# Four-layer token kernel on one core: inverse roots of layer 0 moved from GpSimd to ScalarE, a shorter QR step, LayerNorm products on GpSimd, rotations spread over three MLP groups

## The chip, the cores and the metric

The kernel runs on one core of one Trainium2 chip. The metric is the device time of one execution in microseconds (us); less is better. Five engines each work through an instruction list of their own: TensorE (PE, with its weight loads as PEld), VectorE (DVE), ScalarE (ACT), GpSimd (POOL) and SyncE (SP), which starts the DMAs. They meet only through semaphores.

## The reference, cut to what matters

The input `x` holds 32 sequences ("tiles" below) of 128 tokens with 144 channels. Four stages follow one another:

```python
def layer0(x, c):                                  # layers 2 and 3 are built alike
    sh_a, sc_a, g_a, sh_m, sc_m, g_m = split(swish(c) @ w_mod + b_mod, 6)
    q, k, v = heads((ln(x) * (1 + sc_a) + sh_a) @ w_qkv + b_qkv)      # 16 heads of 9
    q, k = ln(q, g_q), ln(k, g_k)                  # layer 0 alone: a LayerNorm within each head
    o = softmax(q @ k.T * 9 ** -0.5) @ v
    x = x + g_a * (o @ w_proj + b_proj)
    h = gelu((ln(x) * (1 + sc_m) + sh_m) @ w1 + b1)
    return x + g_m * (h @ w2 + b2)

def layer1(x, cond):                               # the rotations
    U, _ = qr(P)                                   # P is 144 x 64
    R = expm(skew(silu(cond) @ W.T + b))           # one 64 x 64 matrix per sequence
    z = x @ U
    return x + (z @ R - z) @ U.T
```

Layer 2 is attention and MLP without the LayerNorm of q and k; layer 3 has the same attention and a mixture of four experts, two per token.

## The kernel before, in words

The 32 tiles stay on the chip in `X`. Each layer takes them one by one through attention, and in groups of four through the MLP (8 groups a layer). The stages of one tile are, by their names in the code: `ln` and `xh` (LayerNorm statistics and product, for two tiles at a time), `xt` and `xe` (transpose, modulate), `qkv`, `v` (copies out of PSUM), in layer 0 `n1` and `n2` (the LayerNorm of q and k; its means are taken out of the weights beforehand, so that only an inverse root is left), `h1`, `r1` (split in a high and a low part), `qt`, `kt` (transposes), `s1`, `mx` (scores and their maximum), `s2`, `ex` (scores again, exponential), `pv`, `oe` (weighted values), `pj`, `py` (projection, gate). A group's MLP is `mln`, `mxh`, `mxt`, `mxe`, `mxs`, `up`, `ue` (gelu), `dn`, `de`.

Beside layer 0 run three further pieces of work. The QR of `P` is 64 Householder steps, each dependent on the one before: `qb` on PE broadcasts a row (L1831), `qc` on ACT copies it to `VS` and sums its squares (L1198, L1199), `q1` is a dot product and a sign on DVE (L1550, L1551) and the root of the sum on POOL by `pow` (L998), `q2` is six linked DVE instructions (L1558 to L1567). After the 64 steps a chain of small products (`qm` to `qu`, L1842 to L1862 on PE, L1572 to L1591 on DVE) makes U. The matrix exponential is 12 squarings (`sq`, L1907 on PE, L1003 on POOL, L1231 on ACT, L1632 on DVE). A rotation (`rxt` to `re`, for four tiles; L1795 to L1821 on PE) needs U, the exponential, and the finished layer 0 of its four tiles; layer 2 of a tile needs its rotation. There are eight rotations, placed by the table `ROTS`: two behind MLP group 6, six behind group 7.

The inverse roots of q and k are made in `n1`: DVE sums the squares (L1374) and scales them (L1376), POOL raises 128x32 numbers to the power -0.5 (L962), DVE multiplies (L1383, L1386). The LayerNorm products are made in part on DVE (128 channels, L1277) and in part on POOL (the last 16 channels, three times, L931).

The order of the instructions on each engine is made when the program is built. `order()` gives every stage a place on a common scale of tiles from the tables PAIR, TILE, GROUP, EXPERT, STEP and START; `plan()` then walks through all engines with costs of its own for each instruction (class `Probe`) and lets each engine take, among its stages that are ready, the one with the lowest place. Each engine's list is fixed from then on. Where PE would have nothing to do in that plan, it puts in filler products of `eye` with `eye`, whose result nobody reads (stage `hum`, L1666). The plan counts one table load of ACT (1300 in its costs) when an exponential follows a gelu or the reverse. ACT_TABLE_LOAD instructions themselves are put in when the program is compiled.

```python
                elif stage == "q2":
                    ...
                    link(e.scalar_tensor_tensor(SH[:, k:k + 1], sc[:, 2:3], -1.0, sc[:, 1:2], ALU.add, ALU.mult))
                    after()
                    link(e.scalar_tensor_tensor(sc[:, 4:5], VS[:, 0:1], SH[:, k:k + 1], sc[:, 0:1], ALU.mult, ALU.add))
                    link(e.scalar_tensor_tensor(sc[:, 6:7], T1[:, k:k + 1], SH[:, k:k + 1], sc[:, 6:7], ALU.mult, ALU.add))
```

## Time and profile before

| | us |
|---|---|
| median of 3 runs (1365.66 to 1374.56) | 1369.18 |
| the profiled execution | 1369.59 |
| its span in the trace | 1367.7 |

The span is the time from the first to the last instruction that the profiler saw; 1.9 us lie around it. Busy time of an engine is the time in which at least one of its instructions ran; the fillers of PE count as busy. PEclk is the TensorE clock that was granted, as a share of full speed. Each row of a group of instructions names its line in the kernel, its engine, the tiles it writes and reads (`s_` in SBUF, `p_` in PSUM, buffer numbers left out), the count, the busy time and the mean duration of one, and the idle time of the engine just before them with what ended it.

### The profile page before, as it was taken

How to read it: one execution, taken by the hardware profiler on the slowest of the kernel's cores; microseconds unless marked ns; L12 is line 12 of the kernel's file. 1: busy time of each engine (PE TensorE's matmuls, PEld its weight loads, DVE VectorE, ACT ScalarE, POOL GpSimd, SP SyncE). 2: the span in 40 equal slices, each digit the busy share in tenths (PEclk: the TensorE clock that was granted, in tenths of full speed). 3: DMA queues.
4: the chain of work that ended last, by engine and by line, in shares of the span. 5: the costliest groups of instructions: out<-in, count | busy, mean ns of one | idle time of the engine just before them, and what ended most of it. 6: DMA issues, size and time to landing. Idle time of an engine off the chain costs nothing. (4 is left out here: it accounts for less than half of the span.)

```text
span 1367.7 us, 36454 instructions
## 1 busy us (share of the span) xinstructions
PE 1285.6 (94%) x13444; PEld 1069.1 (78%) x13444; DVE 957.7 (70%) x2820; ACT 910.3 (67%) x1792; POOL 666.9 (49%) x782
## 2 busy tenths in 40 slices
PE   8898989999999999998999999999999999999998
PEld 7467767777788877676877778778888889888897
DVE  6788788878888746688677777776666656655341
ACT  3664867757767636666776775677867776776641
POOL 5757788988988321132333333244353342515331
PEclk9999989989899899999899999999999999999999
DMA  6321111111121101143121222221111111111100
GB/s 187 95 86 31 44 43 44 47 37 43 37 60 48 54 24 44 45 124 79 59 69 58 65 64 67 58 77 42 37 57 35 53 42 48 53 34 58 44 12 22
DMA packets 98069, 76.15 MB, mean 56 GB/s; under 512 B 25536, under 2 KB 83179, under 8 KB 97766
## 3 DMA queue, kind: packets, MB, share of 16 engines
q1 hardware_dynamic: 97894, 73.83, 19.0%
q8 instruction: 108, 1.77, 0.5%
q14 instruction: 67, 0.55, 0.1%
HBM read 43.27 MB, written 28.95 MB: 53 GB/s over the span
## 5 line engine op out<-in xcount | busy, mean ns | idle before, releaser
L1788 PE MATMUL p_B<-s_pC,s_H 128*128 128x144 f32 x1900 | 250.4, 288 | 0.9 <-ACT s_FA L1020 0.8
L1408 DVE TENSOR_REDUCE s_MX<-p_S 128x16 f32<-128x2048 f32 x96 | 219.4, 2286 | 38.6 <-PE p_S L1720 37.6
L1788 PEld LDWEIGHTS p_B<-s_pC,s_H 128*128 128x128 f32 x1900 | 239.9, 190 | 7.0 <-issue 2.0
L1117 ACT ACTIVATE s_Pm<-p_S 128x2048 f32<-128x2048 f32 x96 | 180.2, 1878 | 25.1 <-PE p_S L1734 24.5
L962 POOL TENSOR_TENSOR s_s<-s_s,s_half 128x32 f32<-128x32 f32 x32 | 175.0, 5471 | 17.2 <-DVE s_s L1376 16.9
L1168 ACT ACTIVATE s_H<-p_B,s_pC 128x512 f32<-128x512 f32 (+1 forms) x207 | 137.8, 686 | 61.5 <-PE p_B L1654 60.2
L958 POOL TENSOR_TENSOR s_OC<-s_OC,s_RB 72x256 f32<-72x256 f32 x96 | 70.6, 736 | 191.1 <-DMA s_RB<-sums 191.0
L1519 DVE SCALAR_TENSOR_TENSOR s_CQ<-p_B,s_rw,s_CQ 128x144 f32<-128x144 f32 x128 | 41.1, 363 | 115.1 <-PE p_B L1788 114.5
L966 POOL TENSOR_TENSOR s_X<-s_X,s_GA 128x144 f32<-128x144 f32 x96 | 48.5, 505 | 138.2 <-DVE s_GA L1427 138.1
L1660 PE MATMUL p_B<-s_eye,s_QK 128*128 128x128 f32 x768 | 111.1, 282 | 2.8 <-ACT s_JS L1199 1.0
L1660 PEld LDWEIGHTS p_B<-s_eye,s_QK 128*128 128x128 f32 x768 | 88.3, 144 | 15.2 <-issue 5.3
L931 POOL TENSOR_SCALAR s_XHA<-s_X,s_MVA,s_VEA 128x48 f32<-128x48 f32 x96 | 52.9, 561 | 88.4 <-PE p_B L1694 87.2
L1743 PE MATMUL p_B<-s_Pm,s_VA 128*32 128x128 f32 x2560 | 90.7, 285 | 1.6 <-ACT s_Pm L1117 0.4
L1654 PE MATMUL p_B<-s_XMh,s_WFh 128*128 128x512 f32 x207 | 90.3, 436 | 0.2 <-DVE s_XMs L1464 0.2
L1654 PE MATMUL p_B<-s_XMl,s_WFh 128*128 128x512 f32 x207 | 82.8, 400 | 0.0
L1654 PE MATMUL p_B<-s_XMs,s_WFs 80*128 80x512 f32 x207 | 82.8, 400 | 0.0
L1654 PE MATMUL p_B<-s_XMh,s_WFl 128*128 128x512 f32 x207 | 82.4, 398 | 0.0
L1743 PEld LDWEIGHTS p_B<-s_Pm,s_VA 128*32 128x32 f32 x2560 | 67.9, 113 | 13.8 <-issue 4.7
L1720 PEld LDWEIGHTS p_S<-s_KT,s_QT 27*128 27x128 f32 x1536 | 51.5, 188 | 33.6 <-ACT s_Pm L1117 17.1
L1734 PEld LDWEIGHTS p_S<-s_QT,s_KT 29*128 29x128 f32 x1536 | 52.6, 191 | 29.7 <-issue 13.2
L1720 PE MATMUL p_S<-s_KT,s_QT 27*128 27x128 f32 x1536 | 64.9, 286 | 9.9 <-ACT s_Pm L1117 8.3
L976 POOL TENSOR_TENSOR s_X<-s_X,s_GM 128x288 f32<-128x288 f32 x48 | 38.5, 808 | 72.4 <-DVE s_GM L1511 36.2
(318 smaller groups left out, 3214.8 us busy)
## 6 DMA issues: line engine op xcount, KB each, us to landing
heads<-s_OT SPq DMA_DIRECT2D x96, 256.0 KB, 2.3
s_GM<-gates SPq DMA_DIRECT2D x48, 144.0 KB, 3.2
s_GA<-gates SPq DMA_DIRECT2D x96, 72.0 KB, 3.0
s_OC<-heads SPq DMA_DIRECT2D x192, 36.0 KB
s_RB<-sums SPq DMA_DIRECT2D x192, 36.0 KB
s_QT<-s_MS SPq DMA_DIRECT2D x192, 8.0 KB
s_SG<-in_main SPq DMA_DIRECT2D x33, 72.0 KB, 2.2
out<-s_X SPq DMA_DIRECT2D x8, 288.0 KB, 3.6
```

Of the source, the lines that this page charges most:

```text
L931: e.tensor_scalar(XH[:, k, 128:208].rearrange("p (a c) -> p a c", c=16)[:, 0:5:2, :], X[:, b, 128:144].unsqueeze(1).to_broadcast([128, 3, ...
L958: e.tensor_tensor(OC[n % 2][0:72, :], OC[n % 2][0:72, :], RB[n % 2][:, :], ALU.mult).then_inc(SEM["ml"], 1)
L962: e.tensor_tensor(s32[n % 2][:, 3, :], s32[n % 2][:, 2, :], half[:, :], ALU.pow).then_inc(SEM["n1p"], 1)
L1117: e.activation(Pm[n % 2][:, :], bank["s2", i][:, :], ACT.Exp, scale=SCALE).then_inc(SEM["ex"], 1)
L1168: e.activation(hb[0:n, to, :], bank["up", i][0:n, :], ACT.Gelu_apprx_tanh, bias=b1[l][0:n, 5 * x + to:5 * x + to + 1]).then_inc(SEM["ge"], 1)
L1408: e.tensor_reduce(MX[n % 2][:, :], bank["s1", i][:, :].rearrange("p (h k) -> p h k", h=NH), AX.X, ALU.max, negate=True).then_inc(SEM["mx"], 1)
L1654: r = e.matmul(o, x if swap else y, y if swap else x, start=(j == 0), stop=(j == 3))
L1660: r = e.transpose(bk[:, 128 * j:128 * j + 128], QK[n % NQK][:, c:c + 128].bitcast(F32), eye[:, :])
L1720: ins = e.matmul(bk[:, c:c + 128], QT[n % NT][q, j, :], KT[n % NT][q, j, :], start=True, stop=True)
L1734: ins = e.matmul(bk[:, c:c + 128], KT[n % NT][q, j, :], QT[n % NT][q, j, :], start=True, stop=True)
L1743: ins = e.matmul(bk[32 * r:32 * r + 32, 128 * j:128 * j + 128], VA[n % NVA][:, h, :], Pm[n % 2][:, 512 * r + 128 * j:512 * r + 128 * j + 1 ...
L1788: ins = e.matmul(bk[:, 256 * i2:256 * i2 + C], hb[0:n, c, 128 * t:128 * t + 128], w2[l][0:n, 5 * x + c, :], start=(c == 0), stop=(c == 4))
```

## The change

- **Inverse roots of q and k (layer 0).** DVE only sums the squares. DVE then makes one Newton step for 1/sqrt in three linked instructions (L1429 to L1433). POOL has no part in it.
- **A 1x1 logarithm** (`lnz`) stands at the start of ACT's program and, in layer 0, ahead of the first softmax exponential or `n1` that follows a gelu.
- **QR step.** ACT sums the squares first (of half the values) and then copies; POOL's root waits only for the sum and writes `SH` itself; the sign goes to a column of `GO` and, with a factor of 0.5, into `sc[:, 2:4]`; `q2` falls from six linked instructions on DVE to four. VS and T1 lie in one tile, so that a single instruction takes both numbers.
- **LayerNorm products of layer 0** (both LayerNorms, 64 products of 128 channels) go from DVE to POOL. Layers 2 and 3 keep them on DVE.
- **Squaring.** POOL's factor 2.0 is read from memory and is no immediate.
- **Rotations.** `ROTS` puts three behind MLP group 5, two behind 6 and three behind 7.
- **Order.** All place tables have new numbers, and two per layer (first and last tile) in place of one; some of the planner's costs are changed (what DVE and POOL cost each other).

```diff
-ROTS = {6: (0, 1), 7: (2, 3, 4, 5, 6, 7)}
+ROTS = {5: (0, 1, 2), 6: (3, 4), 7: (5, 6, 7)}
...
-        more = {ACT.Exp: 95, ACT.Gelu_apprx_tanh: 110, ACT.Identity: 175, ACT.Square: 50 if accum_out is None else 90}[func]
-        return self.part(80 + more + 0.78 * cols(o), {ACT.Exp: "exp", ACT.Gelu_apprx_tanh: "gelu"}.get(func))
+        more = {ACT.Exp: 95, ACT.Ln: 95, ACT.Gelu_apprx_tanh: 110, ACT.Identity: 175, ACT.Square: 50 if accum_out is None else 90}[func]
+        return self.part(80 + more + 0.78 * cols(o), {ACT.Exp: "exp", ACT.Ln: "exp", ACT.Gelu_apprx_tanh: "gelu"}.get(func))
...
+            if p.shared and e == "dve":
+                ns += max(0.0, taken - now)
...
-TILE = {"qkv": (-1.037, -0.643, -0.587), "v": (-2.055, 2.067, 1.367), "n1": (-0.683, 3.714, 10.374), "n2": (-0.114, 4.8, 4.506),
+TILE = {"qkv": (-1.095, -0.958, -0.705, -0.727, -0.31, -0.747), "v": (-3.273, -1.805, 1.958, 4.146, 4.719, 2.995),
...
-            def normal_rest(bs, MV, VE, XH, done):
+            def normal_rest(bs, MV, VE, XH, done, whole):
                 for k, b in enumerate(bs):
+                    if whole:
+                        e.tensor_scalar(XH[:, k, 0:128], X[:, b, 0:128], MV[:, k, 0:1], VE[:, 1, k:k + 1], ALU.subtract, ALU.mult)
...
-                elif stage == "n1":
-                    n = i[0]
-                    w.wait_ge(*at("n1", n))
-                    e.tensor_tensor(s32[n % 2][:, 3, :], s32[n % 2][:, 2, :], half[:, :], ALU.pow).then_inc(SEM["n1p"], 1)
...
+                if stage == "ue":
+                    gelu = True
+                elif stage in ("ex", "n1") and gelu:
+                    gelu = False
+                    if i[0] < B and not isinstance(e, Probe):
+                        e.activation(lnz[:, :], eye[0:1, 0:1], ACT.Ln)
...
+                elif stage == "n1":
+                    n = i[0]
+                    s = s32[n % 2]
+                    w.wait_ge(*at("n1", n))
+                    w.wait_ge("d_small", 32)
+                    e.activation(s[:, 1, :], s[:, 0, :], ACT.Ln, bias=half[:, 32:33], scale=1.0 / HD).then_inc(SEM["n1l"], 1)
+                    w.wait_ge(*at("n1l", n))
+                    e.activation(s[:, 3, :], s[:, 1, :], ACT.Exp, scale=-0.5).then_inc(SEM["n1p"], 1)
...
+                    link(e.scalar_tensor_tensor(s[:, 2, :], s[:, 3, :], -0.5 / HD, s[:, 3, :], ALU.mult, ALU.mult))
+                    after()
+                    link(e.scalar_tensor_tensor(s[:, 2, :], s[:, 0, :], HD * EPS, s[:, 2, :], ALU.add, ALU.mult))
+                    after()
+                    link(e.scalar_tensor_tensor(s[:, 3, :], s[:, 2, :], 1.5, s[:, 3, :], ALU.add, ALU.mult))
...
-                    link(e.scalar_tensor_tensor(SH[:, k:k + 1], sc[:, 2:3], -1.0, sc[:, 1:2], ALU.add, ALU.mult))
-                    after()
-                    link(e.scalar_tensor_tensor(sc[:, 4:5], VS[:, 0:1], SH[:, k:k + 1], sc[:, 0:1], ALU.mult, ALU.add))
-                    link(e.scalar_tensor_tensor(sc[:, 6:7], T1[:, k:k + 1], SH[:, k:k + 1], sc[:, 6:7], ALU.mult, ALU.add))
+                    link(e.scalar_tensor_tensor(sc[:, 4:6], sc[:, 2:4], SH[:, k:k + 1], sc[:, 0:2], ALU.mult, ALU.add))
```

What the build makes of this, on the engines that matter most. In a row, `x12` is a count and the name after `<-` what is read; L numbers are those of the kernel that the row belongs to.

ScalarE, between the copies of a tile of layer 0 and a later softmax exponential, before: COPY s_VA, COPY s_CQ and ACTIVATE s_CS are stage `v`, CAST s_QK is `h1`, s_SC a squaring, s_VS and s_JS a QR step, s_Pm the softmax.

```order
L1071 COPY s_VA<-p_B 128x16x9
L1075 COPY s_CQ<-p_B 128x288
L1078 ACTIVATE s_CS<-p_B 128x288
L1231 ACTIVATE s_SC<-p_B 128x4x64
L1198 COPY s_VS<-p_B 64x131
L1199 ACTIVATE s_JS,s_scq<-p_B 64x131
L1231 ACTIVATE s_SC<-p_B 128x4x64
L1091 CAST s_QK<-s_CQ 128x2x16x18
L1231 ACTIVATE s_SC<-p_B 128x4x64
L1117 ACTIVATE s_Pm<-p_S 128x2048
```

The same engine after, about the same tile:

```order
L1163 ACTIVATE s_Pm<-p_S 128x2048
L1047 ACTIVATE s_FA<-p_B,s_MT 128x128
L1051 ACTIVATE s_FA<-p_B,s_MT 80x128
L1122 ACT_TABLE_LOAD
L1122 ACTIVATE s_s<-s_s,s_half 128x32
L1124 ACT_TABLE_LOAD
L1124 ACTIVATE s_s<-s_s 128x32
L1244 ACTIVATE s_JS,s_scq<-p_B 64x132
L1245 COPY s_T<-p_B 64x132
L1155 CAST s_MS<-p_B 32x128
```

The logarithm and the exponential of a tile each have a table load ahead of them. Over the program ACT has 88 table loads before and 149 after; up to the 28th softmax 13 before and 79 after.

TensorE at the end of the QR, before: L1846 to L1851 are the chain that makes U, L1855 to L1862 its last products, L1666 the fillers, L1803 and L1804 the first rotation's product with U, L1752 and L1753 a projection.

```order
L1846 MATMUL p_B<-s_TB,s_GO 64x64
L1752 MATMUL p_B<-s_pP,s_OC 128x144
L1753 MATMUL p_B<-s_pP,s_OC 128x144
L1850 MATMUL p_B<-s_YB,s_TB 64x64
L1851 MATMUL p_B<-s_TB,s_YB 64x64
L1666 MATMUL p_S<-s_eye 128x128
L1855 MATMUL p_B<-s_T,s_TB 64x64
L1666 MATMUL p_S<-s_eye 128x128
L1860 MATMUL p_B<-s_T,s_YB 128x144
L1861 MATMUL p_B<-s_YB,s_T 128x128
L1666 MATMUL p_S<-s_eye 128x128 x6
L1803 MATMUL p_B<-s_FM,s_U 128x512
```

The same chain after (L1904, L1908 and L1909 are what L1846, L1850 and L1851 were):

```order
L1904 MATMUL p_B<-s_TB,s_GO 64x64
L1716 MATMUL p_B<-s_eye,s_QK 128x128 x12
L1908 MATMUL p_B<-s_YB,s_TB 64x64
L1909 MATMUL p_B<-s_TB,s_YB 64x64
L1800 MATMUL p_B<-s_Pm,s_VA 32x128 x16
L1809 MATMUL p_B<-s_pP,s_OC 128x144
L1810 MATMUL p_B<-s_pP,s_OC 128x144
L1904 MATMUL p_B<-s_TB,s_GO 64x64
L1817 MATMUL p_B<-s_eye,s_XHM 128x128
L1818 MATMUL p_B<-s_eye,s_XHM 80x128
```

The chain moved forward among the tiles' own products. Counted by softmaxes: at the 28th, 52 of the 64 QR steps stood ahead before and all 64 after, and 20 more products of an MLP's first half (one group) after than before; the fillers up to the 28th, the 36th, the 68th softmax and the end were 181, 272, 405 and 417 before, and are 165, 183, 287 and 287 after.

GpSimd in a stretch of layer 0, before: L962 is the root of `n1`, L998 that of the QR, L1003 a squaring's factor, L958 the product with the softmax sums, L966 the sum into X.

```order
L998 TENSOR_TENSOR s_scq<-s_scq,s_halfp 64x1
L958 TENSOR_TENSOR s_OC<-s_OC,s_RB 72x256
L962 TENSOR_TENSOR s_s<-s_s,s_half 128x32
L966 TENSOR_TENSOR s_X<-s_X,s_GA 128x144
L998 TENSOR_TENSOR s_scq<-s_scq,s_halfp 64x1
L1003 TENSOR_SCALAR s_SC<-s_HS 128x4x64 x2
```

And after, where L963 is the new product of 128 channels and L964 the old one of 16:

```order
L1027 TENSOR_TENSOR s_SH<-s_scq,s_halfp 64x1
L963 TENSOR_SCALAR s_XHA<-s_X,s_MVA,s_VEA 128x128
L964 TENSOR_SCALAR s_XHA<-s_X,s_MVA,s_VEA 128x3x16
L963 TENSOR_SCALAR s_XHA<-s_X,s_MVA,s_VEA 128x128
L964 TENSOR_SCALAR s_XHA<-s_X,s_MVA,s_VEA 128x3x16
L1032 TENSOR_SCALAR s_SC<-s_HS,s_half 128x4x64
```

The long root is gone from between the QR's roots, and the products stand in its place.

## Rows read from the trace of the kernel before

**Rows 1.** The page, busy time and share of each engine over the span.

```profile
PE 1285.6 (94%) x13444; PEld 1069.1 (78%) x13444; DVE 957.7 (70%) x2820; ACT 910.3 (67%) x1792; POOL 666.9 (49%) x782
```

**Rows 2.** Stretches: length, busy time (instructions) of each engine, granted clock, DMA.

```profile
50.00:440.00 390.00, 357.20 (x4164) 285.77 (x4164) 323.93 (x1069) 272.08 (x652) 313.16 (x260) 0.94 0.18 50
440.00:478.00 38.00, 35.12 (x376) 29.34 (x373) 27.56 (x108) 27.05 (x59) 14.09 (x23) 0.87 0.20 53
478.00:500.00 22.00, 20.41 (x137) 16.46 (x137) 9.46 (x41) 2.83 (x15) 5.09 (x8) 0.94 0.15 39
500.00:586.00 86.00, 80.44 (x739) 57.84 (x741) 55.36 (x147) 52.75 (x132) 15.95 (x27) 1.00 0.13 38
900.00:1368.00 468.00, 458.99 (x4345) 406.73 (x4343) 262.33 (x703) 310.35 (x459) 177.65 (x259) 1.00 0.15 43
```

**Rows 3.** The same for the fillers alone (L1666): PE busy, PEld busy, then clock.

```profile
50.00:440.00 390.00, 39.38 (x260) 34.76 (x260) 0.94 0.18 50
440.00:586.00 146.00, 25.60 (x162) 21.28 (x162) 0.95 0.15 42
478.00:500.00 22.00, 13.97 (x77) 10.86 (x76) 0.94 0.15 39
586.00:1020.00 434.00, 37.74 (x262) 33.69 (x262) 0.98 0.23 66
```

**Rows 4.** Groups of instructions on ACT, 50 to 440 us.

```profile
L1117 ACT ACTIVATE s_Pm<-p_S 128x2048 f32<-128x2048 f32 x28 | 52.6, 1879 | 13.2 <-PE p_S L1734 13.1
L1199 ACT ACTIVATE s_JS<-p_B 64x140 f32<-64x140 f32 (+43 forms) x44 | 11.6, 263 | 0.0
L1198 ACT COPY s_VS<-p_B 64x140 f32<-64x140 f32 (+43 forms) x44 | 10.7, 244 | 16.1 <-PE p_B L1831 16.1
L1168 ACT ACT_TABLE_LOAD x7 | 9.0, 1283 | 0.1
L1117 ACT ACT_TABLE_LOAD x6 | 7.7, 1283 | 0.1
```

**Rows 5.** ACT in order of time around a table load: start, duration.

```profile
145.31 0.69 ACT L1168 ACTIVATE s_H<-p_B,s_pC 128x512 f32<-128x512 f32 x1 [0.24 <-PE p_B L1654]
146.01 1.28 ACT L1117 ACT_TABLE_LOAD   x1
147.31 1.88 ACT L1117 ACTIVATE s_Pm<-p_S 128x2048 f32<-128x2048 f32 x1
```

**Rows 6.** Groups on ACT over the span: a small exponential.

```profile
L1150 ACT ACTIVATE s_rt<-s_rt 128x16 f32<-128x16 f32 x8 | 1.7, 216 | 11.0 <-DVE s_rt L1479 11.0
```

**Rows 7.** Groups on POOL, 50 to 440 us.

```profile
L962 POOL TENSOR_TENSOR s_s<-s_s,s_half 128x32 f32<-128x32 f32 x30 | 164.2, 5473 | 17.2 <-DVE s_s L1376 16.9
L1003 POOL TENSOR_SCALAR s_SC<-s_HS 128x256 f32<-128x256 f32 x48 | 42.0, 885 | 3.5 <-DVE s_HS L1632 3.5
L931 POOL TENSOR_SCALAR s_XHA<-s_X,s_MVA,s_VEA 128x48 f32<-128x48 f32 x24 | 13.2, 557 | 8.1 <-PE p_B L1694 7.6
```

**Rows 8.** Groups on DVE, 50 to 440 us.

```profile
L1558 DVE SCALAR_TENSOR_TENSOR s_SH<-s_scq 64x1 f32<-64x1 f32 x51 | 11.9, 234 | 2.7 <-POOL s_scq L998 2.6
L1561 DVE SCALAR_TENSOR_TENSOR s_scq<-s_T,s_SH,s_scq 64x1 f32<-64x1 f32 x51 | 12.3, 240 | 0.0
L1277 DVE TENSOR_SCALAR s_XHM<-s_X,s_MVM,s_VEM 128x128 f32<-128x128 f32 x24 | 7.8, 392 | 0.0
L1376 DVE TENSOR_SCALAR s_s<-s_s 128x32 f32<-128x32 f32 x28 | 7.2, 259 | 1.0
L1551 DVE TENSOR_SCALAR s_scq<-s_VS 64x1 f32<-64x1 f32 x51 | 7.2, 141 | 0.0
```

**Rows 9.** DVE, then PE, in order of time at the end of the QR.

```profile
498.21 0.28 DVE L1591 TENSOR_TENSOR s_U<-s_U,s_eye 64x128 f32<-64x128 f32 x1
...
500.04 0.99 PE L1803 MATMUL p_B<-s_FM,s_U 128*128 128x512 f32 x1
```

More of the change, by code:

```diff
@@ L88, in __init__ @@
     def __init__(self, waits, ns, table):
-        self.waits, self.ns, self.table, self.signals, self.size, self.land, self.tiling = waits, ns, table, [], 0, 0, None
+        self.waits, self.ns, self.table, self.signals, self.size, self.land, self.tiling, self.shared = waits, ns, table, [], 0, 0, None, False
     def then_inc(self, sem, by):
@@ L168, in tensor_tensor @@
         if op == ALU.pow:
-            return self.part(400 + 157 * cols(o))
-        return self.lane(cols(o), (110 if cols(o) >= 128 and len(o.shape) < 4 else 0) + SHARED if self.name == "dve" and not (in_psum(x) or in_psum(y)) else 0)
+            p = self.part(400 + 157 * cols(o))
+            p.shared = cols(o) == 1
+            return p
+        both = not (in_psum(x) or in_psum(y)) and len(o.shape) < 4
+        p = self.lane(cols(o), 120 if self.name == "dve" and both and cols(o) >= 128 else 0)
+        p.shared = both or self.name == "pool"
+        return p
     def tensor_scalar(self, o, x, s1, s2, op0, op1=None):
         if self.name == "pool":
-            return self.part(460 + 1.55 * cols(o))
-        return self.lane(cols(o), 0 if isinstance(s1, float) or cols(o) < 32 else 110 if in_psum(x) else 45 + SHARED)
+            p = self.part(460 + 1.55 * cols(o))
+            p.shared = isinstance(s1, float)
+            return p
+        p = self.lane(cols(o), 0 if isinstance(s1, float) or cols(o) < 32 else 110 if in_psum(x) else 45)
+        p.shared = not (isinstance(s1, float) or in_psum(x))
+        return p
     def scalar_tensor_tensor(self, o, x, s, y, op0, op1):
-        return self.lane(cols(o), (0 if cols(o) < 32 else 55) + (0 if in_psum(x) else SHARED))
+        p = self.lane(cols(o), 10 if cols(o) < 32 else 65)
+        p.shared = not in_psum(x)
+        return p
     def tensor_tensor_reduce(self, o, x, y, s, z, op0, op1, acc):
-        return self.lane(cols(x), 20 + SHARED)
+        return self.lane(cols(x), 30)
     def tensor_reduce(self, o, x, axis, op, negate=False):
@@ L200, in dma_start @@
         return p
-SHARED = 75
 MIXED = ("start", "rt")
@@ L334, in advance @@
         running[e] = True
+        if p.shared and e == "dve":
+            ns += max(0.0, taken - now)
+        elif p.shared:
+            taken = now + ns
         if e == "pe":
@@ L421, in put, with lean @@
         at.append((pos, len(at), stage, i))
+    def lean(pos, l, part):
+        return pos[2 * l] + (pos[2 * l + 1] - pos[2 * l]) * part
     def n_pos(n):
@@ L464, in order @@
                 continue
-            put(p + pos[l], name, n)
+            put(p + lean(pos, l, n % B / (B - 1)), name, n)
     free = 0.0
@@ L471, in order @@
         free = p + START["mlp step"][l]
+        group, expert = ({k: lean(v, l, g / (NG - 1)) for k, v in d.items()} for d in (GROUP, EXPERT))
         for stage in ("mln", "mxh", "mxs") + (("rt",) if l == 2 else ()):
-            put(p + GROUP[stage][l], stage, m)
+            put(p + group[stage], stage, m)
         for k in range(G):
-            put(p + GROUP["mxt"][l] + k * STEP["mxt"][l], "mxt", m, k)
-            put(p + GROUP["mxe"][l] + k * STEP["mxt"][l], "mxe", m, k)
+            put(p + group["mxt"] + k * STEP["mxt"][l], "mxt", m, k)
+            put(p + group["mxe"] + k * STEP["mxt"][l], "mxe", m, k)
         ne = NE[LAY[l]]
@@ L576, in program @@
         ltm = sb("ltm", [128, 64])
-        half = sb("half", [128, 32])
+        half = sb("half", [128, 34])
         halfp = sb("halfp", [128, 1])
+        lnz = sb("lnz", [1, 1])
         WQ, WF, wp, packC, packP, w2, b1 = {}, {}, {}, {}, {}, {}, {}
@@ L1197, in scalar_program @@
                         w.wait_ge(*at("q2a", k - 1))
+                    e.activation(JS[:, 0:C - k], bank["qb", i][0:64, 0:C - k], ACT.Square, scale=0.5, accum_out=sc[:, 0:1]).then_inc(SEM["qc"], 1)
                     e.copy(VS[:, 0:C - k], bank["qb", i][0:64, 0:C - k]).then_inc(SEM["qc"], 1)
[L1199 removed]
                 elif stage == "qv":
@@ L1997, in layout @@
     a["eye2"] = np.concatenate([np.eye(64, dtype=f)] * 2, 0)
-    a["half"] = np.full((128, 32), -0.5, f)
+    a["half"] = np.concatenate([np.full((128, 32), -0.5, f), np.full((128, 1), EPS, f), np.full((128, 1), 2.0, f)], 1)
     lt = np.zeros((4, 4, 4), f)
```

120 lines of the change are left out of this document (67 added, 53 removed), and 21 rows, old and new, of the table TILE.

## Prediction

> **What bounds the kernel now.** I read the busy shares first, then the stretches of time, then inside the stretches the groups of one engine. Over the whole span PE is busy 94% and no other engine more than 70% [rows 1], but part of PE's busy time is filler. From 900 us on it is really PE: 459.0 of 468 us busy, with ACT at 310.4, that is 66% [rows 2]. Nothing of the change can speed up that stretch. Layer 0 looks otherwise. From 50 to 440 us (28 softmaxes, [rows 4]) PE is busy 357.2 of 390 us, of which 39.4 us are fillers [rows 2, 3], so its real work fills 81%; DVE has 323.9 (83%), POOL 313.2 (80%), ACT 272.1 (70%) [rows 2]. Three engines at 80 to 83% that hand work to each other in a fixed order leave no engine as the one bound: each waits a little for the others. From 440 to 586 us, with eight more softmaxes, layer 0 ends, the QR ends and the rotations run. Inside it lie 22 us (478 to 500) in which ACT is busy 2.8 us, and 14.0 of PE's 20.4 busy us are fillers [rows 2, 3]: the serial end of the QR. The last DVE instruction of that chain begins at 498.21, the first rotation's product with U at 500.04 [rows 9].
>
> **The change, part by part.** The sum is made against the profiled execution, 1369.6 us (span 1367.7 and 1.9 around it); the median of the runs is 0.4 lower, which I neglect.
>
> *POOL.* 32 roots of 5.47 us go: -175 us [rows 7]. 64 products of 128x128 come. No row shows one on POOL; the nearest are 0.557 us for 128x48 and 0.885 us for 128x256 [rows 7], so each is between these, and I take 0.70: +45 us. The new factor read from memory has the size of the old one and I leave it at 0.885. POOL falls from 80% to about half of the stretch; its waiting roots of the QR no longer stand behind a 5.5 us instruction.
>
> *DVE.* 64 products at about 0.39 go (-25 us), two linked QR instructions of 0.234 and 0.240 go and one of 0.141 comes (64 times, -21 us), the scaling of 0.259 goes (32 times, -8 us) [rows 8]. Three Newton instructions on 128x32 come, 96 in all; the nearest row in size is the 0.259 of L1376: +25 us. In sum about -29 us. These two engines gain nothing on the path by themselves; they cease to hold the others.
>
> *ACT.* The logarithm and exponential of a tile each need a table load, because the program as built loads two different tables: 149 loads against 88, and 79 against 13 up to the 28th softmax (the section on the change). A load lasts 1.283 us [rows 4]. A load of before began at 146.01, and the exponential behind it at 147.31: beside the load itself nothing is lost [rows 5]. So 66 x 1.283 = 84.7 us come to ACT in this stretch. The 56 small activations have no row; the nearest is 0.216 us for 128x16 [rows 6]; I take 0.22: 12 us. Twelve QR steps that stood behind the 28th softmax now stand ahead of it, with 0.244 + 0.263 us and the reading of the sum: about 8 us [rows 4]. ACT's work in the stretch becomes 272 + 85 + 12 + 8 = 377 us, 97% of the 390. The planner counts no load between logarithm and exponential, so the fixed order has not made room for them. How full can an engine be here? Before, the fullest was DVE with 83%; with POOL and DVE relieved I take 88% for ACT: 377 / 0.88 = 428 us, **+38 us**. The bounds: if ACT can run without gaps, 0; at 80%, the share that POOL has now, 471 us, +81. On one tile alone the new way is shorter, 2 x 1.28 + 2 x 0.22 + 3 x 0.26 = 3.8 us against 5.47 + 0.26 = 5.7, which speaks for the low end; that ACT also serves PE (copies out of PSUM, softmax) speaks for the high end.
>
> The Trainium skill ("ScalarE: Activation LUTs", section on what ACT_TABLE_LOAD costs) adds a drain of about 1.38 us to each load, about 2.66 us in all. By that the stretch would get 66 x 1.38 = 91 us more on ACT. The trace does not agree: 0.02 us lie between the load and the next activation [rows 5].
>
> *End of layer 0.* Between the 28th and 36th softmax the list of PE had 91 fillers and has 18 now (the section on the change). A filler costs 25.6 us / 91 = 0.28 us [rows 3], so 73 of them are 20 us, plus a few us of real idling beside them (PE idles 1.6 of the 22 us, and 2.9 + 5.6 in the rest, [rows 2]): 22 us. This is safe as far as the order goes, since the chain that makes U now stands among products of tiles, and the chain of 64 steps is over by the 28th softmax. Moreover the QR steps (12) and one MLP group that now stand earlier take with them about 13 us of PE work, which fit in the stretch before where ACT is the limit (PE's real work there is 318 of 390 us). Together **-35 us**. The lower bound of this gain is 15 (the fillers of 478 to 500 us, 14.0 [rows 3], alone), the upper 45 (all fillers and idle time of the 146 us, 25.6 + 10.1, and half of the moved work). What is late next there is PE itself.
>
> *Layer 2.* Its fillers between the 36th and 68th softmax fall from 133 to 104. The 586 to 1020 us stretch shows 37.7 us for them [rows 3], 0.28 each: **-8 us** (bounds 0 and -15, since nothing but the order has changed there).
>
> *Sum.* 1369.6 + 38 - 35 - 8 = 1364.6; I say **1364 us**.
>
> **The rivals.**
>
> A, the loads are hidden. ACT waits for 118 of the 390 us now, the loads and activations fill 105 of them, and the relief of DVE and POOL is what counts. ACT's term is then about 0 to +5: 1369.6 + 2 - 38 - 8 = 1326 us. For it: the shorter way of one tile, the long POOL root gone, loads that may stand in a wait (an ACT load before a waiting activation costs nothing). Against it: 97% busy is more than any engine but PE shows, and PE only where it has no one to wait for [rows 2].
>
> B, slower: ACT becomes the bound of layer 0. One mechanism: the two loads delay all that stands behind them on ACT (QR copy, K and Q copies, softmax), PE runs out of finished copies and idles, and ACT in turn waits for PE. Layer 0 to the 28th softmax then takes what ACT's 377 us take at 80%: 471, +81 us, and the sum is 1369.6 + 81 - 35 - 8 = 1407 us. It decides below a share of 87%, where ACT's term eats both gains, and it is over 1% slower below 84%. For it: the three fullest engines of layer 0 stop at 80 to 83% today. Against: ACT would be alone at its limit, and they are three.
>
> C, slower, by the clock: PE's granted clock is 0.94 in the stretch of layer 0 and 1.00 from 500 to 586 us [rows 2]. If PE idles more, it is granted the half rate (1.2 for 2.4 GHz) more often. At 0.94 some 12% of the stretch is at half rate; at 30% of it, 70 us more are at half rate and up to 35 us of PE's work are lost, on top of the forecast: 1399 us.
>
> D, the change does not do what its planner says of it, in the good sense: one table serves both functions. Then 61 of the loads are not there or cost nothing and ACT gets 20 us: 1326 us as in A. The Trainium skill (same page, section on table sets) says that a set holds both exponential and logarithm, so that a logarithm and an exponential need one load. The rows of the built program show a load ahead of each of the two, so this has little weight; the skill's drain has as little.
>
> **How the numbers follow.** The forecast's own range is a share of ACT between 92% (410 us: 1346) and 85% (444 us: 1380): chance 0.42, of which 0.14 below 1355.5. A: 0.26. B: 0.23. C: 0.05. D: 0.02. The drain at its full price, a slower kernel too: 0.02. About 1% is what a measurement of this kernel can tell from no change, so: faster by over 1% 0.14 + 0.26 + 0.02 = 0.42, within 1% 0.28, slower by over 1% 0.23 + 0.05 + 0.02 = 0.30. The range that should hold it 8 times in 10 reaches over most of A (to 1326) and up to B's 1405, where the share of ACT is 80%.
>
> **What would show it.** In the new profile: 149 table loads of 1.28 us, two per tile of layer 0; POOL about half busy there and DVE some 75%; ACT between 85 and 92% busy from 50 us to the 28th softmax, which ends between 460 and 495 us; no stretch like 478 to 500 with ACT idle and PE on fillers; the first product with U before the 32nd softmax. Right for A would be the 28th softmax at 440 or earlier with ACT at 95%; for B at over 500, with PE's idle time put down to ACT's copies and softmax; for C the same with a clock below 0.90. The forecast is wrong in its base if the 36th softmax comes no less than 140 us after the 28th (the QR was not what held that stretch), or if layers 2 and 3 differ by more than 15 us.

## The result and the profile after

The changed kernel takes 1435.37 us (median of 4 runs, 1432.78 to 1442.92), the kernel before, on the same chip, 1367.42 us (4 runs, 1361.61 to 1374.56). The ratio is 1.050, with an interval of 1.044 to 1.057: slower by 68 us, where 1364 us were forecast and the range ended at 1405. One later run of the kernel before, at 1378.95 us and a lower granted clock (0.961 against 0.969 to 0.982 in the other six of its set), counts as slow and is left out of every median and ratio below. The profiled execution of the changed kernel took 1442.9 us (span 1441.1), 7.5 us above its median.

Where the time went is read first from one instruction that every tile has, the softmax exponential (128x2048, L1117 before, L1163 after). Its starts, in us from the start of the span:

| | 28th (layer 0, last quarter) | 36th (layer 2 has begun) | 68th (layer 3 has begun) | end |
|---|---|---|---|---|
| before | 415.6 | 574.5 | 888.8 | 1367.7 |
| after | 525.7 | 645.2 | 956.0 | 1441.1 |
| after, less before, within the stretch | +110.1 | -39.4 | -3.5 | +6.2 |
| forecast for the stretch | +38 | -35 | -8 | 0 |

So the end of layer 0 and the two later layers came out near the forecast, and one term failed: what ACT's added work, the table loads above all, costs on the way to the 28th softmax. The stretches between these points, before, with the columns of [rows 2]:

```profile
50.00:415.60 365.60, 333.74 (x3942) 265.13 (x3943) 303.08 (x1006) 254.25 (x609) 292.13 (x242) 0.93 0.18 50
415.60:574.50 158.90, 148.76 (x1335) 116.19 (x1335) 104.06 (x340) 93.63 (x234) 53.47 (x70) 0.96 0.15 42
```

and after:

```profile
50.00:525.70 475.70, 406.28 (x4090) 317.15 (x4089) 326.15 (x1114) 368.20 (x816) 205.91 (x291) 0.81 0.15 41
525.70:645.20 119.50, 109.12 (x1060) 81.43 (x1060) 71.56 (x198) 79.93 (x174) 37.05 (x56) 0.97 0.20 52
645.20:956.00 310.80, 280.24 (x3300) 231.36 (x3302) 236.47 (x584) 213.03 (x386) 98.59 (x155) 0.96 0.25 71
956.00:1441.10 485.10, 472.96 (x4471) 416.15 (x4471) 271.71 (x737) 312.74 (x472) 185.28 (x272) 0.99 0.15 43
```

The fillers alone (L1722 after; PE and PEld), first before, for the two stretches of layer 0:

```profile
50.00:415.60 365.60, 34.39 (x223) 30.36 (x224) 0.93 0.18 50
415.60:574.50 158.90, 28.15 (x182) 23.51 (x182) 0.96 0.15 42
```

and after:

```profile
50.00:525.70 475.70, 29.79 (x174) 26.30 (x174) 0.81 0.15 41
525.70:645.20 119.50, 5.30 (x36) 4.59 (x36) 0.97 0.20 52
```

The reader is to see three things. ACT has 368.2 us of work from 50 us to the start of the 28th softmax, 114 more than the 254.2 of before (105 more were forecast); but it is busy only 77% of the stretch, less than every share considered, the 80% of rival B included. POOL and DVE are far from their limits (43% and 69%). And PE, which has almost the same instructions plus the moved ones, is busy for 376.5 us without its fillers (406.3 - 29.8) against 299.4 before, idles for 69.4 us against 31.9, and does this at a granted clock of 0.81 against 0.93. No engine is full in this stretch.

ACT's table loads, 50 to 526 us, after (to set beside the last two of [rows 4]; five lines issue them, 73 loads where there were 12 up to 415.6 us before):

```profile
L1124 ACT ACT_TABLE_LOAD x29 | 37.2, 1283 | 0.5
L1122 ACT ACT_TABLE_LOAD x26 | 33.4, 1283 | 0.5
L1214 ACT ACT_TABLE_LOAD x7 | 9.0, 1283 | 0.1
L1061 ACT ACT_TABLE_LOAD x7 | 9.0, 1283 | 0.1
L1163 ACT ACT_TABLE_LOAD x4 | 5.1, 1283 | 0.0
```

One pair in order of time (start, duration; to set beside [rows 5]), and what ACT does a few us later:

```profile
195.57 0.26 ACT L1244 ACTIVATE s_JS<-p_B 64x120 f32<-64x120 f32 x1 [0.24 <-PE p_B L1889]
...
196.09 1.28 ACT L1122 ACT_TABLE_LOAD   x1
197.38 0.32 ACT L1122 ACTIVATE s_s<-s_s,s_half 128x32 f32<-128x32 f32 x1
197.72 1.28 ACT L1124 ACT_TABLE_LOAD   x1
199.01 0.23 ACT L1124 ACTIVATE s_s<-s_s 128x32 f32<-128x32 f32 x1
199.15 0.44 ACT L1047 ACTIVATE s_FA<-p_B,s_MT 128x128 f32<-128x128 f32 x1
...
209.38 0.26 ACT L1244 ACTIVATE s_JS<-p_B 64x119 f32<-64x119 f32 x1 [2.62 <-PE p_B L1889]
...
211.27 0.59 ACT L1169 COPY s_OT<-p_B 128x512 f32<-128x512 f32 x1 [1.40 <-PE p_B L1800]
```

Around the pair ACT runs without a gap: the copies of `FA` that stand behind the pair follow at once, 2.6 us later than they could without it. Ten us later ACT itself waits 2.62 and 1.40 us for PE. So it goes through the whole stretch: the loads push work back, and the time does not come back out of ACT's waits, since those are for PE. Whether PE is late by the same loads this view alone does not say; the experiments do.

The longest waits, 50 to 525.7 us, after (engine, tile, line, whom it waits for: total us, times, longest):

```profile
POOL s_SH L1027 <- ACT s_JS L1244: 126.1, 43, 12.4
...
DVE s_GO L1604 <- ACT s_T L1245: 36.6, 27, 3.2
DVE s_s L1429 <- ACT s_s L1124: 31.8, 19, 3.2
```

The POOL wait costs nothing by itself: POOL has nothing else to do. The DVE wait for the exponential of `n1` (31.8 us in 19 waits) shows DVE's list standing behind the loads. PE shows the same. Summed over all its waits in this stretch, its idle time ended with a result of ACT for 55.7 of 69.4 us, against 15.8 of 31.9 before.

### The profile page after: what moved, and what is told of

Its sections match the earlier page's. It is cut to its first block, busy times and chain, and to the rows that moved or that the text cites. A ratio compares the mean times of both kernels' runs of the same rounds, so it can differ in the third digit from the quotient of the medians.

```text
span 1441.1 us, 35990 instructions
## 1 busy us (share of the span) xinstructions
PE 1311.0 (91%) x13184; PEld 1077.7 (75%) x13184; DVE 937.1 (65%) x2757; ACT 1003.1 (70%) x1926; POOL 546.8 (38%) x814
## 4 chain that ended last, share of the span: by engine, by line
PE 58%; ACT 13%; DVE 9%; issue 9%; DMA 4%; SPq 4%; POOL 3%; DVEq 0%; POOLq 0%; ACTq 0%
PE p_B L1710 17%; PE p_B L1846 13%; PE p_B L1800 4%; PE p_B L1716 4%; DVE s_MX L1460 3%; PE p_S L1791 3%; ACT s_Pm L1163 2%; PE p_S L1777 2%; PE p_B L1965 2%; ACT L1122 2%; PE p_B L1809 2%; PE p_S L1710 1%; DMA sums<-s_RD 1%; PE p_B L1810 1%; DMA s_RB<-sums 1%
## 5 line engine op out<-in xcount | busy, mean ns | idle before, releaser
L1846 PE MATMUL p_B<-s_pC,s_H 128*128 128x144 f32 x1880 | 249.3, 289 | 1.8 <-ACT s_T L1245 1.7
L1846 PEld LDWEIGHTS p_B<-s_pC,s_H 128*128 128x128 f32 x1880 | 239.0, 191 | 7.3 <-ACT s_T L1245 2.2
L1163 ACT ACTIVATE s_Pm<-p_S 128x2048 f32<-128x2048 f32 x96 | 180.1, 1876 | 34.2 <-PE p_S L1791 33.5
L1716 PE MATMUL p_B<-s_eye,s_QK 128*128 128x128 f32 x764 | 127.5, 305 | 5.9 <-ACT s_CS L1116 1.6
L1716 PEld LDWEIGHTS p_B<-s_eye,s_QK 128*128 128x128 f32 x764 | 98.9, 157 | 19.6 <-issue 6.1
L1800 PE MATMUL p_B<-s_Pm,s_VA 128*32 128x128 f32 x2688 | 98.4, 291 | 6.2 <-ACT s_Pm L1163 4.0
L1027 POOL TENSOR_TENSOR s_SH<-s_scq,s_halfp 64x1 f32<-64x1 f32 x64 | 36.9, 576 | 143.3 <-ACT s_JS L1244 143.3
L1800 PEld LDWEIGHTS p_B<-s_Pm,s_VA 128*32 128x32 f32 x2688 | 73.9, 116 | 20.7 <-issue 10.9
L1169 ACT COPY s_OT<-p_B 128x512 f32<-128x512 f32 x84 | 49.0, 583 | 52.7 <-PE p_B L1800 52.5
L1791 PE MATMUL p_S<-s_QT,s_KT 29*128 29x128 f32 x1536 | 70.0, 302 | 13.5 <-DVE s_MX L1460 7.6
L1791 PEld LDWEIGHTS p_S<-s_QT,s_KT 29*128 29x128 f32 x1536 | 56.0, 203 | 34.8 <-issue 14.1
L964 POOL TENSOR_SCALAR s_XHA<-s_X,s_MVA,s_VEA 128x48 f32<-128x48 f32 x96 | 53.4, 565 | 56.6 <-PE p_B L1751 56.5
```

The source lines that it names most:

```text
L964: e.tensor_scalar(XH[:, k, 128:208].rearrange("p (a c) -> p a c", c=16)[:, 0:5:2, :], X[:, b, 128:144].unsqueeze(1).to_broadcast([128, 3, ...
L1163: e.activation(Pm[n % 2][:, :], bank["s2", i][:, :], ACT.Exp, scale=SCALE).then_inc(SEM["ex"], 1)
L1169: e.copy(OT[n % 2][:], bank["pv", i][:, :]).then_inc(SEM["oe"], 1)
L1716: r = e.transpose(bk[:, 128 * j:128 * j + 128], QK[n % NQK][:, c:c + 128].bitcast(F32), eye[:, :])
L1791: ins = e.matmul(bk[:, c:c + 128], KT[n % NT][q, j, :], QT[n % NT][q, j, :], start=True, stop=True)
L1800: ins = e.matmul(bk[32 * r:32 * r + 32, 128 * j:128 * j + 128], VA[n % NVA][:, h, :], Pm[n % 2][:, 512 * r + 128 * j:512 * r + 128 * j + 1 ...
```

## The experiments

Theory after the result: **every us of loads that the fixed order did not foresee is a us at the end**, since each engine works its list in order and waits for the others at every stage. Rivals: the loads are a small part and the new order or the moved instructions cost the rest; a load hurts in a way that other ACT work does not; and the low clock of PE (rival C) is itself the cause. All ratios are to the kernel before on the same chip (1369.5, 1361.6 and 1364.1 us in the three sets of runs). The same kernel thus differs by up to 8 us from set to set, and so much is uncertain in a difference in us between changed versions of different sets.

**One set for both functions.** The changed kernel with every list in the same order; only the loads differ. Ahead of the first `n1` or exponential behind a gelu, the combined set is loaded by hand, and the build then adds no load of its own between logarithm and exponential.

```diff
-                        e.activation(lnz[:, :], eye[0:1, 0:1], ACT.Ln)
+                        e.add_instruction(mybir.InstLoadActFuncSet(name=nc.get_next_instruction_name(), engine=mybir.EngineType.Activation, act_func_set_id=6))
```

> The changed kernel with the same order on every engine, but the dummy logarithms are replaced by an explicit load of the one table set that holds both logarithm and exponential, so that the program has 82 table loads and not 149. Theory L (the two loads per tile, which the order made no room for, cost the time): layer 0 up to the 28th softmax falls from 526 us to about 420, the run lies between 1310 and 1350 us. Rival O (the order itself, the products on GpSimd or the clock are at fault, the loads only use ACT's idle time): less than 25 us are won, 1410 us or more.

Measured: 1352.87 us, ratio 0.988 (0.982 to 0.993). 82 loads in place of 149: 67 x 1.283 = 86.0 us of load time less, and 82.5 us less than the changed kernel (86.0 less by the spans of the profiled executions). That is 2.9 us above the top of the range expected, and the 28th softmax starts at 444.2, not at 420. The stretches to the 28th softmax, and from there to the 36th:

```profile
50.00:444.20 394.20, 361.06 (x4062) 282.76 (x4061) 317.61 (x1099) 287.32 (x736) 204.97 (x290) 0.90 0.17 48
444.20:558.80 114.60, 109.08 (x1073) 81.43 (x1072) 71.66 (x198) 76.23 (x170) 37.66 (x57) 0.99 0.20 54
```

In the first stretch there are 14 loads for 73, and from the start of the program 15 for 79: 64 x 1.283 = 82.1 us less of them, and the 28th softmax starts 81.5 us earlier. Without its fillers (25.4 us here) PE is busy 335.6 us, 40.9 less than after, and idle 33.1, 36.3 less. PE's idle time ended by ACT falls from 55.7 to 12.4 us, and DVE's wait for the exponential of `n1` from 31.8 to 0.7:

```profile
L1435 DVE SCALAR_TENSOR_TENSOR s_s<-s_s 128x32 f32<-128x32 f32 x28 | 5.5, 197 | 0.7 <-ACT s_s L1130 0.7
```

ACT's own idle time is the same in both: 107.5 us after, 106.9 here (111.4 before). The loads used next to none of it. So the loads explain the whole loss, and this version is the fastest of all: 1.2% below the kernel before, with an interval clear of 1.

**The loads alone.** The kernel before, in its own order, with the logarithm and the exponential of one number behind `v` of each tile of layer 0, whose results nobody reads.

```diff
+                            e.activation(lnz[:, 0:1], eye[0:1, 0:1], ACT.Ln)
+                            e.activation(lnz[:, 1:2], eye[0:1, 0:1], ACT.Exp)
```

> The kernel before with its order, plus a logarithm and an exponential of a single number on ACT behind the copies of each tile of layer 0, which no one reads: 150 table loads in place of 88. Theory L: the same 62 loads (80 us of ACT) cost here nearly what they cost in the changed kernel, 60 us or more: 1430 to 1470 us. Rival O: the order before has enough idle ACT time (118 of 390 us), 20 us or less: below 1390 us.

Measured: 1464.27 us, ratio 1.071 (1.066 to 1.076). The two groups of loads over the span:

```profile
L1081 ACT ACT_TABLE_LOAD x32 | 41.1, 1283 | 0.6
L1082 ACT ACT_TABLE_LOAD x32 | 41.1, 1283 | 0.2
```

ACT's busy time rises from 910.3 to 997.4 us (+87; some loads of before are no longer needed), the span by 93.4. Nothing else of the change is in this kernel: the order, POOL's roots and the QR are as before. Its stretch to the 28th softmax (start 509.6) looks like that of the changed kernel:

```profile
50.00:509.50 459.50, 384.38 (x3982) 302.56 (x3981) 308.81 (x1024) 333.08 (x730) 299.19 (x246) 0.82 0.14 40
```

The clock is 0.82 and ACT 72% busy, with no other engine fuller than before by its share. That is the picture of rivals B and C together, made by loads alone: they bring the clock from 0.93 to 0.82. The 28th softmax starts 94.0 us later than before, so the whole loss arises up to there.

**Is a load special?** The same place and kernel, but five activations of 64x384 per tile and no load.

```diff
+                            for k in range(5):
+                                ...
+                                e.activation(GO[:, :, :].rearrange("p a b -> p (a b)"), eye[0:64, 0:1].to_broadcast([64, 384]), ACT.Square).then_inc(SEM["pad"], 1)
```

> The kernel before with its order, plus five activations of 64x384 that nobody reads on ACT behind the copies of each tile of layer 0: about 2.5 to 3.0 us of ACT a tile (80 to 95 us in all) and no table load. Theory T (any ACT time that the order has no room for moves the end by as much, a table load is nothing special): 70 to 100 us more, 1440 to 1470 us. Rival S (a table load costs more than its own 1.28 us, or stops something else): less than half of what the loads cost, below 1415 us.

Measured: 1456.33 us, ratio 1.070 (1.066 to 1.074).

```profile
L1083 ACT ACTIVATE s_GO<-s_eye 64x384 f32<-64x384 f32 x160 | 83.5, 522 | 4.0
```

83.5 us of plain ACT work (ACT's busy time rises by 76.7, since neighbours overlap a little) cost 94.8 us by the medians and 86.3 by the spans. A load is nothing special; it is 1.28 us of ACT.

**The same on DVE.** Again the kernel before in its order, with two reductions of 1.47 us per tile on DVE, at the end of `n2` (the stage of DVE's multiplications L1383 and L1386).

```diff
+                        for k in range(2):
+                            ...
+                            e.tensor_reduce(scr[:, q:q + 2], eye[:, 0:1].unsqueeze(2).to_broadcast([128, 2, 640]), AX.X, ALU.max)
```

> The kernel before with its order, plus two reductions of 128x1280 that nobody reads on DVE behind the scaling of each tile's q and k in layer 0, about 1.4 us each, some 88 us of DVE in all. If it is the fixed order that lets every engine's extra time through, DVE (83% busy) passes on 80% or more of it: 1440 us or more. If ACT is a special case because it frees PE's banks, DVE passes on less than half: below 1410 us.

Measured: 1438.99 us, ratio 1.058 (1.053 to 1.062).

```profile
L1391 DVE TENSOR_REDUCE s_scr<-s_eye 128x2 f32<-128x1280 f32 x64 | 91.8, 1473 | 0.0
```

91.8 us on DVE (its busy time rises by 76.9) cost 77.4 us by the medians, 70.3 by the spans: about 0.8 us each, or 0.9 by the busy time. The median lies 1 us below the 1440 set for that expectation. DVE was the fuller of the two before (83% of the stretch to ACT's 70%), and yet it forgave a little more. In these runs the fuller engine was not the dearer one. The work stood at another place of the tile than on ACT, so how much of the difference is the engine's and how much the place's is not shown.

**Is it the clock?** The changed kernel, order unchanged, with nine more filler products per tile of layer 0, three each ahead of `s1`, `s2` and `pv`, to keep the clock up.

```diff
+                    if i[0] < B and not isinstance(e, Probe):
+                        for _ in range(3):
+                            e.matmul(bk[:, 0:128], eye[:, :], eye[:, :], start=True, stop=True)
```

> The changed kernel with nine more filler products per tile of layer 0 on PE (three ahead of what s1, s2 and pv wait for), 288 in all, about 42 to 85 us of PE work at full or half rate. Theory C (a good part of the loss is PE at its lower clock, because it waits: granted clock 0.81 up to the 28th softmax): the clock there rises above 0.88 and the time falls by 10 us or more, below 1425. Rival W (the waits alone are the loss, and PE has no time to give): the clock may rise, the time does not fall, 1435 to 1480 us.

Measured: 1471.34 us, ratio 1.077 (1.072 to 1.082). The 28th softmax starts at 546.3:

```profile
50.00:546.30 496.30, 434.91 (x4602) 358.01 (x4601) 327.23 (x1114) 367.25 (x817) 205.95 (x291) 0.90 0.14 39
```

The clock does rise, from 0.81 to 0.90, and the kernel is 36 us slower still. In this stretch PE's other work falls from 376.5 to 326.2 us, but the fillers rise from 29.8 to 108.7: here they cost more than the clock they buy. The low clock makes PE's own work longer and so is part of how the loads act, but it follows from the loads (0.93 to 0.82 in the run with the loads alone), and this cure does not undo it.

**The same fillers on the version with one set.**

> The same nine fillers per tile in the changed kernel with one table set (1353 us, clock 0.90 in the stretch). If the clock is worth more than the fillers cost there too: below 1345 us, which would be the best version; if not, 1353 to 1390 us.

Measured: 1388.91 us, ratio 1.018 (1.014 to 1.023); 36 us slower than without them here too, at a clock of 0.985 over the run (0.954 without). The price is about the same whether the loads are there or not.

**A planner that knows of the loads.** The changed kernel, but the costs of the planner count a load of 1300 at each change between logarithm and exponential, so that all lists are made anew.

```diff
-        return self.part(80 + more + 0.78 * cols(o), {ACT.Exp: "exp", ACT.Ln: "exp", ACT.Gelu_apprx_tanh: "gelu"}.get(func))
+        return self.part(80 + more + 0.78 * cols(o), {ACT.Exp: "exp", ACT.Ln: "ln", ACT.Gelu_apprx_tanh: "gelu"}.get(func))
```

> The changed kernel with a planner that charges both loads, so that a new order and new fillers are made with them in view; 155 loads stay. Theory L1 (it is that the order did not count on the loads): half or more of the loss comes back, 1400 us or less. Theory L2 (it is ACT's own time on the way of each tile, whoever plans it): within 20 us of the changed kernel, 1415 to 1450 us.

Measured: 1448.73 us, ratio 1.058 (1.055 to 1.061), with 155 loads. Over the whole run nothing came back. The stretches say more. The first line below goes up to the 28th softmax, the second from the 36th to the 68th, which is layer 2:

```profile
50.00:481.20 431.20, 375.39 (x4049) 293.53 (x4047) 317.17 (x1104) 362.20 (x809) 199.59 (x283) 0.88 0.15 44
617.50:962.60 345.10, 298.84 (x3294) 244.80 (x3291) 233.95 (x584) 216.50 (x383) 105.53 (x163) 0.90 0.22 60
```

With all its loads this kernel reaches the 28th softmax 44.5 us earlier than the changed kernel. ACT is busy 84% of the stretch, and its idle time is 69.0 us where it was 107.5. Layer 2, to which the edit brings nothing, then takes 345.1 us for 310.8. So in layer 0 something did come back, and it was lost again in layer 2. How much of the 44.5 us is due to the loads being counted, and how much to the order merely being another one, is not shown: a control below moves the 28th softmax by 15 and another by 30 us.

**The root back on POOL.** The changed kernel with `pow` on POOL for the inverse root (DVE scales, no logarithm, no Newton step), lists made anew.

```diff
+                    e.tensor_tensor(s32[n % 2][:, 3, :], s32[n % 2][:, 2, :], half[:, 0:32], ALU.pow).then_inc(SEM["n1p"], 1)
...
-                    e.activation(s[:, 1, :], s[:, 0, :], ACT.Ln, bias=half[:, 32:33], scale=1.0 / HD).then_inc(SEM["n1l"], 1)
```

> The changed kernel with the inverse root of q and k by power on GpSimd as before, no Newton step, 82 table loads; QR step, products on GpSimd, rotations and place tables as changed. Theory L: layer 0 is no longer held by ACT, but GpSimd now has the roots (175 us) and the products (45 us): 1340 to 1385 us. Rival O: 1400 us or more, since order and products stay.

Measured: 1464.17 us, ratio 1.069 (1.063 to 1.074). This has 82 loads and should have been near the version with one set; it is 111 us above it, and outside the range expected. That could be POOL's 5.47 us roots in the way of its new products, or the new order.

**The root alone, and the products back on DVE.** The kernel before with only the root moved to ACT (one set, Newton step), and the version with one set with the LayerNorm products of layer 0 back on DVE (`normal_rest(..., False)`), both with lists made anew.

> The kernel before with only the inverse root of q and k moved to ACT (logarithm, exponential, Newton step on DVE), served by one table set; place tables, QR step, products and rotations as before, a new plan. It adds 0.55 us to ACT and some 0.5 us net to DVE per tile and takes 5.5 us from GpSimd. If GpSimd's root held layer 0, 1335 to 1355 us; if layer 0 is held by ACT and DVE alone, 1370 us or more.

> The changed kernel with one table set, as in the first experiment (1353 us), but the 64 LayerNorm products of layer 0 on DVE as before; the plan is made anew. If the products on GpSimd are a gain, 10 us or more slower than 1353; if GpSimd's 0.7 us against DVE's 0.39 us on the way of a tile is a loss, faster, 1340 or less.

Measured: 1405.89 us, ratio 1.033 (1.029 to 1.038), and 1425.96 us, ratio 1.048 (1.043 to 1.053). Both slower, by 44 and 73 us against the kernel that each was made from. They also have more table loads than it, 102 for 88 and 90 for 82. Four rebuilt orders in a row were bad, whatever they held, so the order itself came under suspicion.

**The order alone.** Two controls in which no instruction but fillers and table loads can change: a constant of the planner is moved a little and all lists are made anew. First the kernel before:

```diff
-SHARED = 75
+SHARED = 80
```

> A control for all runs whose plan is made anew: the kernel before with one cost of its planner changed from 75 to 80 ns (SHARED), no instruction added or removed. If place tables hold for more than the one plan they were made with: within 1% of 1367 us. If a new plan from the same tables is a loss by itself: 20 us or more slower, and then the runs with the root on GpSimd, the root alone and the products on DVE say little of those parts.

then the version with one set:

```diff
-HOP = {"pe": 200, "act": 145, "dve": 115, "pool": 100, "sp": 60}
+HOP = {"pe": 200, "act": 150, "dve": 115, "pool": 100, "sp": 60}
```

> The same control on the other side: the changed kernel with one table set and one cost of the planner (ACT's hop) changed from 145 to 150 ns. Tables robust: within 1% of 1353 us. Tables fitted to one plan: 20 us or more slower, as the run with the products on DVE was (1426).

Measured: 1430.14 us, ratio 1.048 (1.043 to 1.054), where an equal kernel would have 1.000; and 1394.34 us, ratio 1.021 (1.017 to 1.025), 41 us above the version that it was made from. In the first the planner puts in 519 fillers where it had put in 417, and there are 94 loads for 88; in the second 313 fillers for 287 and 86 loads for 82. So the place tables fit one plan each, and a rebuilt order alone costs 41 to 66 us in these two cases. The four runs before these differ by 13 us (the planner that knows, from the changed kernel), 111 us (the root back on POOL, from the version with one set), 44 us (the root alone, from before) and 73 us (the products on DVE, from the version with one set), and at 41 to 66 us for the order alone it may be most of each.

The stretches show where a new order loses. From the starts of the softmaxes, in us:

| | 28th | 28th to 36th | 36th to 68th (layer 2) | 68th to end |
|---|---|---|---|---|
| before | 415.6 | 159.0 | 314.3 | 478.9 |
| one set | 444.2 | 114.6 | 309.5 | 486.9 |
| planner that knows | 481.2 | 136.4 | 345.1 | 484.0 |
| root back on POOL | 467.2 | 152.2 | 360.6 | 473.8 |
| root alone | 437.4 | 138.9 | 320.7 | 504.9 |
| products on DVE | 457.6 | 126.7 | 360.7 | 479.8 |
| control, before | 445.8 | 143.0 | 343.7 | 493.1 |
| control, one set | 429.3 | 120.2 | 355.1 | 489.2 |

The edits of these runs bring nothing to layer 2 but, in some, two more table loads. Yet the rebuilt orders take 321 to 361 us for it, where every kernel that has the order of before or after takes 309 to 315. In the second control layer 0 is even 9 us shorter up to the 36th softmax. So the times of whole runs say nothing reliable on the parts of the change.

## Why the prediction was wrong

**The step that failed** is the ACT term: "How full can an engine be here? Before, the fullest was DVE with 83%; with POOL and DVE relieved I take 88% for ACT". The work under it was nearly right (114 us more where 105 were forecast). The share was wrong: 77% after, 73% with one set, 72% in the kernel before with the loads alone. Dividing work by a share treats ACT's 118 idle us as room, of which I let the loads use most. In this fixed order they are not room: ACT's idle time is 111.4 us before, 107.5 after and 106.9 with one set, and it grew to 126 when loads or plain work were added to the kernel before. ACT is idle because what it waits for is not there yet, in an order that is fixed when the program is built; 85 us more of ACT work delay PE, DVE and POOL, and each delay arrives back at ACT as a later input. Three runs with unchanged lists put the price at about 1 us per us on ACT: 86.0 for 86.0 (one set), 93.4 for 87.1 (loads alone), 86.3 for 76.7 to 83.5 (plain activations), all by spans. At a price of 1 the sum would have been 1369.6 + 66 x 1.283 + 12 + 8 - 35 - 8 = 1431 us; measured were 1442.9 in the profiled execution and 1435 in the median. The prediction had the premise in hand ("the fixed order has not made room for them") and did not use it in the number. A share of 84% does occur, in the kernel whose planner counted the loads.

A smaller slip stands beside it: the stretch from 50 to 440 us holds 28 exponentials, but the 28th starts at 415.6, so 24 us of the 390 lay behind the point that I scaled. ACT's work up to that start was 254 us, not 272. The share that was there before is 70% either way, and the term would have been (254 + 105) / 0.88 - 366 = 42 us for 38.

**Rival B** (+81 for the stretch, 1407 in all) had the mechanism: loads delay what stands behind them on ACT, PE runs out of copies, ACT waits for PE. Its sign was seen too (28th softmax over 500 us, PE's idle time put down to ACT: 55.7 of 69.4 us). Its condition was wrong. It was to decide by ACT's share reaching a limit at 80%, and against it I held that "ACT would be alone at its limit, and they are three". ACT never came to a limit, and the price was paid at every load.

**Rival C.** The clock fell from 0.93 to 0.81, and PE's real work grew by 77.1 us. Some 36 of them are there already with one set (335.6 - 299.4 us, at 0.90, about 13 of it, by the estimate in the prediction, the 12 QR steps and the MLP group that stand earlier); the other 40.9 come and go with the loads, and with them the clock. So about half of the loads' price of 81.5 us appears as longer products (40.9 us, and 4.4 in the fillers) and half (36.3 us) as idle PE. The rival was too small by itself (+35) and is not independent: the same loads make both halves.

**Rivals A and D.** A is out: nothing was hidden. (Its sum takes 38 us for the end of layer 0 where the forecast takes 35; that decides nothing.) D asked whether one table serves both functions. As built it does not: 149 loads, as forecast. But the Trainium skill ("ScalarE: Activation LUTs", section on table sets) names a set with both, and the run with one set bears it out: with that set loaded by hand, 82 loads are left. That run came out at 1352.9; A and D had 1326.

**The drain.** The Trainium skill (same page, section on what ACT_TABLE_LOAD costs) has about 2.66 us for a switch. The trace does not agree: the logarithm begins 0.01 us behind its load (196.09 + 1.28, 197.38) and the whole of 67 loads is worth 82.5 us, that is 1.23 us each.

**What was right.** End of layer 0: -39.4 us for -35. The fillers between the 28th and 36th softmax fell from 28.2 to 5.3 us, 22.9 for the 22 forecast with some idle time in them; PE's idle time did not fall (10.1 us before, 10.4 after), and its other work fell by 16.8 us for 13. (The prediction divided the fillers of 440 to 586 us, of which there are 81, by the 91 between the softmaxes; one costs 0.31 us, not 0.28.) And the first rotation product with U starts at 534.3, ahead of the 32nd softmax (576.5):

```profile
L1861 PE MATMUL p_B<-s_FM,s_U x16: 590/592/697, 534.3 to 639.6; 128*128 128x512 f32 x16
```

Layer 2: -3.5 for -8, and the last stretch +6.2 for 0, both inside the 15 us set as a limit. The shares of POOL and DVE in layer 0 came out lower than foreseen (43% for half, 69% for 75). The durations that had no row, 50 to 525.7 us:

```profile
L963 POOL TENSOR_SCALAR s_XHA<-s_X,s_MVA,s_VEA 128x128 f32<-128x128 f32 x26 | 22.0, 846 | 9.6 <-PE p_B L1751 9.2
...
L1032 POOL TENSOR_SCALAR s_SC<-s_HS,s_half 128x256 f32<-128x256 f32 x48 | 46.4, 968 | 39.2 <-DVE s_HS L1688 39.2
```

```profile
L1122 ACT ACTIVATE s_s<-s_s,s_half 128x32 f32<-128x32 f32 x29 | 9.3, 320 | 0.3
L1124 ACT ACTIVATE s_s<-s_s 128x32 f32<-128x32 f32 x29 | 6.6, 229 | 0.3
```

```profile
L1429 DVE SCALAR_TENSOR_TENSOR s_s<-s_s 128x32 f32<-128x32 f32 x29 | 6.2, 215 | 31.8 <-ACT s_s L1124 31.8
L1431 DVE SCALAR_TENSOR_TENSOR s_s<-s_s 128x32 f32<-128x32 f32 x29 | 5.9, 202 | 1.0
L1433 DVE SCALAR_TENSOR_TENSOR s_s<-s_s 128x32 f32<-128x32 f32 x29 | 7.8, 268 | 1.0
```

The product on POOL is 0.846 us (estimate 0.70, bounds 0.557 and 0.885), the logarithm 0.320 and the exponential 0.229 (estimate 0.22), the Newton instructions 0.215, 0.202 and 0.268 (estimate 0.26). The squaring's factor, which I "leave at 0.885", takes 0.968 when it is read from memory. None of these matters to the end.

**What stays open.** Without the superfluous loads the rest of the change is worth 1.2% (1369.5 to 1352.9): the 28th softmax comes 28.6 us later than before, the 36th 15.7 us earlier. How that splits over the roots, the QR step, the products on POOL and the rotations is not known, since taking one out makes a new order. Leaving a part out inside a frozen order was not tried. Nor was a set of place tables tuned for a planner that counts the loads. The run with such a planner was ahead of the changed kernel by 44.5 us at the 28th and 27.7 us at the 36th softmax, so how much of the loads a good plan could hide is open.

## What to carry to other kernels

In a kernel whose engines work fixed lists and hand each other every stage, idle time of an engine is not room for work that the order did not foresee. Price such work at its full length, and look for a reason to go below that. Before logarithm and exponential are used in turns, count the table loads of the built program; where each function brings a load, load the set that has both by hand. And where changing one part makes all lists anew, first run a control that makes them anew and changes nothing: here that alone moved the time by 3 and 5%, while all of the change without its superfluous loads was worth 1.2%. And compare such runs by stretches: a loss in a layer that the edit does not concern is the order's.
